# The scatters of the experts' outputs add to the base rows in the transfer itself, and the gathers of base rows are gone

## The reference

```python
x = x + attention(layernorm(x), ctx, ctx, lengths)         # 8 heads, lengths set the softmax's scale
y = layernorm(x)                                           # 1024 tokens of 256
probs = softmax(y @ Wg); eidx = argmax(probs); gate = probs[eidx]
pos = how many tokens before this one (it included) chose expert eidx, minus 1
keep = pos < C                                             # C = 128 rows for each of 8 experts
xd[eidx * C + pos] = y, dropped where not keep
h = silu(xd @ W1) * (xd @ W3)                              # 256 -> 352, for each expert
oe = h @ W2                                                # 352 -> 256
out = oe[eidx * C + pos] * gate * keep
shared = (silu(y @ sw1) * (y @ sw3)) @ sw2
x = x + out + shared
```

## Time and profile before

| | |
|---|---|
| median of 3 runs | 159.66 us (159.27 to 159.71) |
| the profiled execution's own time | 160.15 us |
| its span | 158.3 us, granted TensorE clock 0.996 of full |
| PE busy | 147.8 us (93%) |
| DVE busy | 99.3 us (63%) |
| ACT busy | 81.6 us (52%) |
| POOL busy | 67.6 us (43%) |
| gathers L475 | 8, mean 1212 ns on POOL |
| scatters L482 | 8, mean 1055 ns on POOL |
| DVE `expert_out` L699 | 8, mean 482 ns |

### The profile page before, as it was taken

One profiled execution on the slowest core, in us unless ns is written; L12 is line 12 of the kernel. 1 busy time (PEld: TensorE's weight loads), 2 busy tenths in 40 slices (PEclk: granted clock), 3 DMA queues, 4 the chain that ended last, 5 costly groups with the idle time before them and its releaser, 6 DMA issues.

```text
span 158.3 us, 3414 instructions
## 1 busy us (share of the span) xinstructions
PE 147.8 (93%) x1256; PEld 99.2 (63%) x1256; DVE 99.3 (63%) x232; ACT 81.6 (52%) x179; POOL 67.6 (43%) x100
## 2 busy tenths in 40 slices
PE   7999999989999999999999999999798999999940
PEld 2465555455556555554554778678695987999720
DVE  0599886688786878875222547877572368776220
ACT  3544364755747485746676267644301585663300
POOL 7124949106409050503969300065700068728650
PEclk9999999999999999999999999999999999999998
DMA  3992716271342600000430099512438402221210
GB/s 79 346 354 75 233 42 206 77 242 39 115 160 68 206 2 4 0 6 0 148 134 2 2 326 315 183 48 86 162 119 237 139 33 83 67 66 64 96 60 33
DMA packets 15824, 18.42 MB, mean 116 GB/s; under 512 B 1980, under 2 KB 15077, under 8 KB 15808
## 3 DMA queue, kind: packets, MB, share of 16 engines
q1 hardware_dynamic: 14368, 14.98, 29.8%
q0 software_dynamic: 1152, 2.97, 5.7%
q10 hardware_dynamic: 288, 0.26, 0.5%
HBM read 14.12 MB, written 4.21 MB: 116 GB/s over the span
## 4 chain that ended last, share of the span: by engine, by line
PE 77%; DMA 8%; DVE 6%; issue 2%; ACT 1%; POOL 1%; SPq 1%; POOLq 0%; DVEq 0%
PE bank L995 18%; PE bank L1032 11%; PE bank L1016 9%; PE bank L1243 5%; PE bank L1096 5%; PE bank L1097 5%; PE bank L1184 4%; DMA out<-xs 4%; PE bank L947 3%; PE bank L1046 3%; PE bank L1218 2%; PE bank L1219 2%; DMA xs<-in_x 2%; DMA xs<-out,rk 2%; PE bank L1058 2%
## 5 line engine op out<-in xcount | busy, mean ns | idle before, releaser
L536 DVE TENSOR_REDUCE nm<-bank 128x2 f32<-128x512 f32 x64 | 40.8, 684 | 10.3 <-PE bank L995 10.3
L789 ACT ACTIVATE pt<-bank 128x512 f32<-128x512 f32 x64 | 34.5, 589 | 15.8 <-PE bank L1016 15.6
L1016 PE MATMUL bank<-qz,kz 32*128 32x256 f32 x256 | 40.8, 402 | 0.0
L995 PE MATMUL bank<-kz,qz 32*128 32x256 f32 x256 | 35.1, 403 | 0.2 <-DVE qz L513 0.2
L995 PEld LDWEIGHTS bank<-kz,qz 32*128 32x128 f32 x256 | 21.9, 184 | 13.0 <-issue 7.2
L1016 PEld LDWEIGHTS bank<-qz,kz 32*128 32x128 f32 x256 | 24.9, 184 | 4.5 <-ACT pt L789 2.8
L1032 PE MATMUL bank<-pt,vext 128*32 128x256 f32 x256 | 20.2, 391 | 0.0
L381 POOL TENSOR_SCALAR qz<-xs,rs,mrs 128x256 f32<-128x256 f32 x14 | 7.7, 562 | 20.0 <-DVE mrs L507 20.0
L460 POOL DMA_INDIRECT expert_rows<-rk,idx_s x8 | 8.3, 1037 | 18.4 <-DVE rk L626 16.5
L475 POOL DMA_INDIRECT xs<-out,rk x8 | 9.7, 1212 | 14.5 <-DMA out<-xs 12.3
L947 PE MATMUL bank<-onesb 128*128 128x512 bf16 x34 | 11.4, 477 | 1.0 <-POOL onesb L375 1.0
(11 more groups left out here) (155 smaller groups left out, 304.4 us busy)
## 6 DMA issues: line engine op xcount, KB each, us to landing
wraw<-in_w SPq DMA_DIRECT2D x10, 352.0 KB, 3.4
wlate<-in_w SPq DMA_DIRECT2D x6, 352.0 KB, 4.6
wraw<-in_w SPq DMA_DIRECT2D x10, 128.0 KB, 3.4
expert_rows<-zero SPq DMA_DIRECT2D x1, 1032.0 KB, 6.2
out<-xs SPq DMA_DIRECT2D x8, 128.0 KB, 3.4
xs<-in_x SPq DMA_DIRECT2D x3, 256.0 KB, 4.9
cs<-in_ctx SPq DMA_DIRECT2D x3, 256.0 KB, 5.4
wlate<-in_w SPq DMA_DIRECT2D x6, 128.0 KB, 4.3
```

The lines of the kernel that those rows point to most:

```text
L536: nc.vector.tensor_reduce(nm[:, b % 2, :, place], scores_bank[:].rearrange("p (u c) -> p u c", u=2), AX_X, ALU.max, negate=True).then_inc( ...
L789: nc.scalar.activation(pt[:, g % NPT, n % 4, :], sc_bank[n % NS][:], ACT.Exp).then_inc(exped, 1)
L995: mm = nc.tensor.matmul(scores_bank[:, u * D:(u + 1) * D], qz[rows, b, half, u * P:(u + 1) * P], kz[rows, b, half, :], start=True, stop=True)
L1016: mm = nc.tensor.matmul(sc_bank[n % NS][:, c * D:(c + 1) * D], kz[rows, b, half, c * P:(c + 1) * P], qz[rows, b, half, :], start=True, sto ...
```

## The change

The eight gathers, their semaphores and DVE's wait for them go away. DVE writes `y * gate` to a new tile `weighed` (8 KB in each partition) instead of adding in place, and the scatter carries `compute_op=ALU.add`: the transfer itself reads the row that stands in `out`, adds the weighed row and writes the sum back. The condition that all base rows have landed stays, now ahead of the first scatter.

```diff
-        res = xs
...
+        weighed = sb("weighed", [P, E, D], F32)
...
-        gathered = [sem(f"gathered{e}") for e in range(E)]
...
             pool.wait_ge(base_stored, 16 * B)
-            for i, (a, z) in enumerate(LOADS):
+            for i in range(len(LOADS)):
                 pool.wait_ge(ld_xe[i], 16)
-                for e in range(a, z):
-                    nc.gpsimd.indirect_dma_start(
-                        res[:, e, :], None, out_rows, number(e),
-                        bounds_check=B * P - 1, oob_is_err=False).then_inc(gathered[e], 16)
-            for e in range(E):
-                pool.wait_ge(gathered[e], 16)
             for e in range(E):
                 pool.wait_ge(e_out, e + 1)
                 nc.gpsimd.indirect_dma_start(
-                    out_rows, number(e), res[:, e, :], None,
-                    bounds_check=B * P - 1, oob_is_err=False).then_inc(out_sent, 16)
+                    out_rows, number(e), weighed[:, e, :], None,
+                    bounds_check=B * P - 1, oob_is_err=False, compute_op=ALU.add).then_inc(out_sent, 16)
             pool.wait_ge(out_sent, 16 * E)
...
             def expert_out(e):
-                dve.wait_ge(gathered[e], 16)
                 dve.wait_ge(e_down, e + 1)
-                nc.vector.scalar_tensor_tensor(res[:, e, :], y_bank[(e + 1) % 2][:, 0:D], xe[:, e, D + 1:DW],
-                                               res[:, e, :], ALU.mult, ALU.add).then_inc(e_out, 1)
+                nc.vector.tensor_scalar(weighed[:, e, :], y_bank[(e + 1) % 2][:, 0:D], xe[:, e, D + 1:DW],
+                                        None, ALU.mult).then_inc(e_out, 1)
```

## The result

The changed kernel takes 160.36 us (median of 5 runs, 160.27 to 160.49) against 159.27 us of the kernel before in the same five rounds (159.14 to 159.71). The ratio is 1.0061, with a 95% interval from 1.0043 to 1.0079. So it is slower by about 1 us: inside the range that was forecast, 159.0 to 162.2, but neither the "no change" that I held likeliest nor inside that case's own stretch, 159.2 to 160.15.

What follows compares the result with a forecast made beforehand. PE, busy 93% of the span, and the tail behind it were taken as the bound. Last scatter's issue ending 0.46 us earlier and landing 0.80 later gave +0.34: 159.66 to 160.0 us, range 159.0 to 162.2.

Steps and rivals of the forecast that it cites:

- no change: Likeliest case for the whole kernel: median 160.0 us, its own stretch 159.2 to 160.15 us; chance 0.42.
- the signs: Wrong if last POOL row to span end stays near 3.9 us or exceeds 5.5, or POOL's row exceeds 1.2 us.
- The stall goes: At PE's `expert_down(1)`: PE no longer waits through DVE for the first gather, -0.51 us, with 0.75 us of slack.
- DVE's output: DVE's `expert_out` for the last two experts: 0.06 us from its shorter form, 0.06 from the missing wait instruction.
- POOL's gathers: Eight gather rows of 1212 ns in the mean leave POOL; nothing behind them was late, so they gain 0.
- The scatter's issue: POOL's row for each accumulating scatter grows by g = 0.10 us, bounds 0 and 0.49, counted twice at the end.
- The landing: Last scatter's way to its landing grows by d = 0.80 us: 0.40 for moving, 0.4 for reading in DRAM.
- The sum: Whole kernel: -0.46 + 0.80 = +0.34 us, giving 158.64 us of span and a median of 160.0 us.
- Fetch, then write: Last scatter: engines fetch rows of `out` before writing and POOL's row grows; 160.2 to 161.8 us, chance 0.25.
- Row by row: Last scatter: each engine finishes one row before the next, eight times 0.4 us, 3.2 us; 162.4 us, chance 0.13.
- Nearly free: Last scatter: the old rows' fetch is hidden, g = 0 and d under 0.15; 159.03 to 159.2 us, chance 0.20.

Runs made afterwards that it cites:

- the second profile: The kernel before, profiled again with no edit: span 157.5 us; median 159.30 us, ratio 1.0006 to before.

## Why the range held and the sum did not

The time lies in the range because the range was wide, from a free addition to a whole gather ahead of the scatter. The mechanism failed by two of the signs that I had named: POOL's row grew beyond 1.2 us (1.54), and the stretch from the last POOL row to the end stayed near 3.9 us (4.1, where I expected 4.7), though the kernel was not faster by 0.4%. The terms, one by one:

**The stall goes, -0.51 us: wrong.** This step failed first. The stall and its slack were read rightly (in the changed kernel `rows_low(4)` ends at 130.27 and PE goes on at 131.02, 0.75 us of slack as forecast), but it was read from one execution, whose own time stood 0.49 us over the median, as I had noted, without asking which of its waits made it so. In the second profile there is no gap at `expert_down(1)`, and moving the wait away left the median where it was. The term is 0 in most executions. The base did not hold either: the sum was added to a median of 159.66 us from three runs, and the kernel before took 159.27 in the rounds with the changed one.

**DVE's output, -0.12 us: half right.** The new form is no shorter: 0.48 us, where the nearest rows had given 0.42. The missing wait instruction is worth what was forecast: DVE starts 0.02 us behind PE (149.81 to 149.83) and not 0.09, so 0.07 us.

**POOL's gathers, 0: wrong by 0.66 us.** They cost nothing where they run, but each leaves 82 ns for the DRAIN at the open end. I had taken the 3.0 us behind the last data for a constant. That is the change's whole gain in most executions, beside 0.07 us, and the version with plain scatters shows it: 158.55 us.

**The scatter's issue, g = 0.10: mis-sized.** It is 0.57 us, over even the upper bound of 0.49. Gather and scatter being alike on POOL said nothing about an addition. Nor did "half as many descriptors again": the profile has 128 data packets for it where a plain scatter has 32. At 0.14 us for 64 rows the 96 more would be some 0.2 us (an estimate); where the rest of the 0.57 us comes from is open. It counts twice, as forecast: scatter 7 starts 152.95 - 149.83 = 3.12 us behind the output of expert 6 and not 152.63 - 150.06 = 2.57 as in the second profile of before, and its own row is longer by 0.57.

**The landing, d = 0.80: right in size.** From the end of POOL's row to the landing it is 3.9 - 1.54 = 2.4 us now, and 2.4 - 0.97 = 1.4 before: 0.9 us. Its parts were not right: the moving grew by about 0.9 us, not by 0.4, and no separate later landing is left to explain. The Trainium skill's rule (Collectives: The Full Stack, the section on the bandwidth ceiling), two source reads for one, gives an estimate of 0.8 us of moving, twice the plain scatter's 0.4; the trace shows 1.4, so it understates this transfer.

**The sum.** By the measured terms: 0.55 + 0.57 for g, 0.9 for d, -0.07 for the wait and -0.66 for the DRAIN make +1.29 us. The two like profiles differ by 158.6 - 157.5 = 1.1, and the experts in the changed one began 0.14 us earlier (PE's first up matmul at 120.42 against 120.56), which I take for variation. The medians differ by 1.09. So the forecast of +0.34 had a gain that was mostly not there (0.51 for the stall, 0.05 for DVE's form), a gain unseen (0.66), and additions priced at 0.17 + 0.80 us where they cost 2.02: 0.34 + 0.56 - 0.66 + 1.05 = 1.29. That these partly cancelled is luck.

**The rivals.** "Fetch, then write" had 0.25 and the range from 160.2 to 161.8 in which the result lies. Its mechanism is not shown: half the bytes took 0.5 us off the moving of 1.4, and no run tells a fetch that comes first from one that is interleaved. Its size is nearer to the truth than the likeliest case. "Row by row" had each row pay a latency of its own, 3.2 us in all. That is excluded: the data moved for 1.4 us, and with as many rows and half the bytes for 0.9. It was right in one thing, that each row goes as a packet by itself. "Nearly free" is excluded.

## What to carry to other kernels

An operation moved into a transfer is cheap while other work covers it and at full price in the last one: here six additions cost nothing and the last two 1.8 us together. Price a change's ends apart from its body, and look in the profile at what the engines' sequencers still do behind the last wait. Before a stall read in one execution enters a sum, compare that execution's own time with the other runs; where it stands above them, the stall may be the reason.

## What the runs showed of the hardware

The DRAIN at the end of POOL's stream takes about 65 ns and 82 ns for each indirect transfer issued since the last DRAIN (24: 2033 ns, 18: 1538, 17: 1457, 16: 1354 to 1380, 8: 691 to 727, 6: 532, 4: 364), and a DRAIN put into an idle stretch, behind the landing of the transfers, takes that time off the end: 159.12 to 158.38 us with one, 159.16 to 157.81 with two. No run has such a DRAIN ahead of the landing.

An accumulating indirect transfer of 128 rows of 1 KB holds POOL for 1.54 us against 0.97, and its data moves for 1.4 us against 0.4, in 128 packets of 1 KB against 32 of 4 KB. The Trainium skill (DMA: Bandwidth & Descriptors, the section on the anatomy of a DMA issued from GpSimd) calls the writing of descriptors small and variable. POOL's whole row is 0.97 of the 2.4 us to the landing in a plain scatter and 1.54 of 3.8 in an addition; no run here tells how much of a row is descriptors.

POOL's rows are longer where DVE's `expert_low` was already running when they began: the first addition, begun 0.18 us behind it, took 2.15 us and the others 1.53 to 1.58. The next three additions had `expert_low` beside them too, but it began some 0.2 us behind them. The first gather took 1.65 us begun 0.15 us behind `expert_low(3)`, and 1.05 us in the profile where it began first. Why is not shown.
